# The experts' weighted products go to a buffer in SBUF and are summed in a step of their own, and the steps are put in another order

## The reference

```python
xn = layernorm(x)
# attention: 16 heads of 64, rotary embedding on q and k, causal mask
q, k, v = split(xn @ W_qkv)
q, k = rotary(q), rotary(k)
attn = softmax(where(mask, q @ k.T / 8, -1e9)) @ v @ W_out
# second block: 16 heads of 8 without a mask, then a gated choice among 8 experts
q, k, v = xn @ Wq + bq, xn @ Wk + bk, xn @ Wv + bv
h = xn + layernorm(softmax(q @ k.T / sqrt(8)) @ v @ Wo + bo, g1, be1)
gate = softmax(h @ Wg + bg)                 # 8 probabilities a row
top_vals, top_idx = top_k(gate, 2)
all_out = einsum('bsd,edf->bsef', h, We) + bexp
moe = sum(top_vals * all_out[top_idx])      # two experts a row
out = x + attn + (h + layernorm(moe, g2, be2))
```

## Time and profile before

| | us |
|---|---|
| three runs | 1206.92, 1212.21, 1213.35 |
| median | 1212.21 |
| the profiled execution, its own time | 1212.86 |
| its span on the core | 1211.0 |
| mean granted PE clock of the span, share of full speed | 0.963 |

### The profile page before, as it was taken

The page is one execution under the profiler, slowest core; times in us unless marked ns, Lnnn a source line. Parts: engine busy times, 40 slices in busy tenths (PEclk is TensorE's granted clock), DMA queues, the critical chain, the costliest instruction groups (busy, mean ns, idle before and its releaser), DMA issues.

```text
span 1211.0 us, 24662 instructions
## 1 busy us (share of the span) xinstructions
PE 1086.8 (90%) x8858; PEld 680.9 (56%) x8858; DVE 858.8 (71%) x2267; ACT 828.8 (68%) x1761; POOL 816.2 (67%) x753
## 2 busy tenths in 40 slices
PE   4688989999898998999988899998999999899996
PEld 3255656556574565756556455654656556565465
DVE  6666686766768568775879758786687776668557
ACT  4487766686657767588674877658776687566772
POOL 2675867587665688577775877649578568755780
PEclk9698999999889999999999999999999999699999
DMA  6112221122111132022211122112221122112111
GB/s 186 41 47 60 68 60 59 54 66 92 45 45 60 47 89 69 27 69 86 76 35 37 60 86 86 32 46 81 69 69 40 51 61 81 30 48 58 66 41 33
DMA packets 64741, 74.30 MB, mean 61 GB/s; under 512 B 22374, under 2 KB 34408, under 8 KB 64620
## 3 DMA queue, kind: packets, MB, share of 16 engines
q1 hardware_dynamic: 61148, 69.79, 18.6%
q10 hardware_dynamic: 3472, 2.95, 0.8%
HBM read 22.64 MB, written 3.67 MB: 22 GB/s over the span
## 4 chain that ended last, share of the span: by engine, by line
PE 63%; ACT 13%; DVE 12%; issue 4%; DMA 2%; POOL 2%; SPq 1%; ACTq 0%; POOLq 0%; DVEq 0%
PE work L1744 11%; PE work L1729 8%; PE work L1756 8%; PE work L1794 7%; DVE fnmax L1496 7%; PE work L1651 6%; ACT fpt L1334 5%; PE work L1653 5%; PE work L1652 5%; ACT pn L1389 4%; PE work L1766 4%; PE work L1775 4%; PE work L1784 3%; PE work L1655 1%; ACT raw L1359 1%
## 5 line engine op out<-in xcount | busy, mean ns | idle before, releaser
L1496 DVE TENSOR_REDUCE fnmax<-work 128x2 fp32r<-128x1024 f32 x256 | 302.3, 1218 | 82.4 <-PE work L1775 81.4
L1231 POOL TENSOR_TENSOR raw<-raw,cos_t 128x512 f32<-128x512 f32 x128 | 164.2, 1283 | 278.1 <-DMA swapped<-raw 275.7
L1389 ACT ACTIVATE pn<-work,nmax 128x512 f32<-128x512 f32 (+3 forms) x512 | 265.4, 537 | 73.8 <-DVE nmax L1609 69.8
L1609 DVE CUSTOM_DVE_ANT_0 work<-work,causal 128x512 f32<-128x512 f32 (+3 forms) x512 | 237.6, 517 | 107.9 <-PE work L1729 107.4
L1334 ACT ACTIVATE fpt<-work 128x1024 f32<-128x1024 f32 x256 | 251.0, 1028 | 76.3 <-PE work L1784 68.6
L1744 PE MATMUL work<-consts,pn 128*128 128x128 f32 x1280 | 182.1, 288 | 16.2 <-ACT fpt L1334 5.7
L1744 PEld LDWEIGHTS work<-consts,pn 128*128 128x128 f32 x1280 | 148.8, 147 | 61.3 <-DVE fnmax L1496 16.6
L1401 ACT COPY pt<-work 128x1024 f32<-128x1024 f32 x128 | 128.9, 1018 | 62.8 <-PE work L1744 62.6
L1235 POOL TENSOR_TENSOR raw<-raw,swapped 128x512 f32<-128x512 f32 x128 | 163.8, 1279 | 10.0
L1246 POOL TENSOR_TENSOR qk_l<-raw,qk_h 128x512 fp32r<-128x512 f32 x128 | 163.1, 1282 | 2.7
L1232 POOL TENSOR_TENSOR swapped<-swapped,sin_t 128x512 f32<-128x512 f32 x128 | 164.3, 1284 | 0.0
(11 more groups left out here) (153 smaller groups left out, 1790.4 us busy)
## 6 DMA issues: line engine op xcount, KB each, us to landing
swapped<-raw SPq DMA_DIRECT2D x256, 128.0 KB, 2.1
l_wide<-l_turned SPq DMA_DIRECT2D x128, 128.0 KB, 2.9
fqs<-fqn SPq DMA_DIRECT2D x96, 128.0 KB
x_in<-in_L_attn_x_dram SPq DMA_DIRECT2D x8, 256.0 KB, 3.9
out_dram<-x_in SPq DMA_DIRECT2D x7, 256.0 KB, 2.5
fpt<-in_L_attn_W_qkv_dram ACTq DMA_DIRECT2D x3, 512.0 KB, 6.4
l_turned<-l_inv SPq DMA_DIRECT2D x64, 16.0 KB
pt<-in_L_ffn_We_dram ACTq DMA_DIRECT2D x1, 512.0 KB, 9.6
```

Of the source, the lines that this page charges most:

```text
L1231: nc.gpsimd.tensor_tensor(raw[:, n % 3], raw[:, n % 3], cos_t[:], ALU.mult)
L1389: ins = nc.scalar.activation(pn[:, h, PN_AT[j]:PN_AT[j] + n], bank_of(("sc", b, c, unit), h)[:, at:at + n], ACT.Exp, scale=-1.0, bias=nmax ...
L1496: nc.vector.tensor_reduce(fnmax[:, g % 2, j * GH + 2 * r:j * GH + 2 * r + 2].unsqueeze(2), bank_of(("fsm", b, g, j), 2 * r, 2).rearrange(" ...
L1609: ins = nc.vector.tensor_tensor_reduce(out=scores, in0=scores, in1=causal[:, S - n:S], scale=-1.0 / math.sqrt(DH), scalar=3.0e38, op0=ALU.add,
```

## The change

1. `moew` is split. The multiplication writes to a new tensor `products` in SBUF, and a new DVE step `msum` sums from there. `FREED` still says `"moe": "moew"`, so it is the multiplication that frees the two banks. There is one `products`: the next multiplication waits for the sum before it. The wait for `x2` moves to the first `msum`.
2. `fnmax` has one copy instead of two; the first `fmax` of a group waits for the landing of `mput` of the group before.
3. `frec` (the reciprocals of `fdiv`) is a view of `stats`; the statistics wait for the last `fdiv`.
4. Six small tensors become views of one, `columns`; the exponent -0.5 is one column, broadcast.
5. `PLACE` and `PSUM` have other numbers (this is most of the diff's lines). In the new order `moew` and `msum` of one tile stand next to each other, as multiplication and sum did.

```diff
-        [168, 171, 172, 173],        # PLACE, "moew", batch 0
+        [168, 172, 174, 176],
+    "msum": [
+        [169, 173, 175, 177],
...
-        singles = sb("singles", [P, 5])
+        columns = sb("columns", [P, 12 * T + 6])
+        scales = columns[:, 0:9 * T].rearrange("p (k n t) -> p k n t", k=3, t=T)
+        spread, shift, rstd = (scales[:, n] for n in range(3))
...
-        fnmax = sb("fnmax", [P, 2, STRIP], F32R)
+        fnmax = sb("fnmax", [P, STRIP], F32R)
...
-        frec = sb("frec", [P, T, GH])
+        products = sb("products", [P, E, D])
+        frec = stats[:, :, 0:GH]
...
+            divided = []
+
             def statistics(kind, n, src):
+                if divided:
+                    dve.wait_ge(done["fdiv"], divided[-1])
...
                     if j == 0:
-                        wait(dve, landed("mput", *ring(2, b, g, G)))
+                        wait(dve, landed("mput", *ring(1, b, g, G)))
...
+                    divided.append(COUNT[x_])
...
                 elif kind == "moew":
                     t = x_[2]
                     if t == 0:
-                        wait(dve, after("x2", b))
                         wait(dve, after("pick", b))
                     wait(dve, after("moe", b, t))
-                    products = bank_of(("moe", b, t), 0, 2).rearrange("p (e d) -> p e d", d=D)
-                    nc.vector.tensor_tensor(products, products, gate_w[:, t].unsqueeze(2).broadcast_to([P, E, D]),
-                                            ALU.mult).then_inc(dve_link, 1)
-                    dve.wait_ge(dve_link, link())
-                    nc.vector.tensor_reduce(branch[:, t].unsqueeze(2), products.rearrange("p e d -> p d e"),
-                                            AX.X, ALU.add).then_inc(done["moew"], 1)
+                    wait(dve, after("msum", *ring(1, b, t, T)))
+                    nc.vector.tensor_tensor(products[:], bank_of(("moe", b, t), 0, 2).rearrange("p (e d) -> p e d", d=D),
+                                            gate_w[:, t].unsqueeze(2).broadcast_to([P, E, D]), ALU.mult).then_inc(done["moew"], 1)
+                elif kind == "msum":
+                    t = x_[2]
+                    if t == 0:
+                        wait(dve, after("x2", b))
+                    wait(dve, after("moew", b, t))
+                    nc.vector.tensor_reduce(branch[:, t].unsqueeze(2), products[:].rearrange("p e d -> p d e"),
+                                            AX.X, ALU.add).then_inc(done["msum"], 1)
                 elif kind == "ln2":
-                    wait(dve, after("moew", b, T - 1))
+                    wait(dve, after("msum", b, T - 1))
```

More of the change, by code:

```diff
@@ L62 @@
         [0],
[L63 to L68, removed]
+        [80],
+        [218],
+        [355],
+        [496],
+        [637],
+        [778],
         [920],
@@ L73 @@
         [88],
[L74 to L79, removed]
+        [229],
+        [368],
+        [513],
+        [654],
+        [793],
+        [935],
     ],
     "tb": [
-        [4],
+        [3],
     ],
     "proj": [
[8 rows of a table removed]
[8 rows of a table added]
     ],
@@ L410 @@
         [145],
[L411 to L412 removed]
+        [274],
+        [403],
         [532],
@@ L439 @@
     "nm2": [
-        [209],
-        [369],
-        [453],
-        [581],
-        [711],
-        [888],
-        [1012],
+        [198],
+        [362],
+        [456],
+        [577],
+        [710],
+        [880],
+        [1010],
         [1037],
@@ L450 @@
         [0],
-        [12],
-        [102],
-        [233],
-        [381],
-        [491],
-        [611],
-        [730],
+        [26],
+        [96],
+        [234],
+        [384],
+        [490],
+        [626],
+        [744],
+    ],
+    "wl": [
+        [1, 6, 20],
     ],
@@ L461 @@
     ],
+    "strl": [
+        [3],
+    ],
     "turn": [
@@ L607 @@
         [139],
-        [266],
-        [394],
-        [519],
-        [646],
-        [775],
-        [901],
-        [995],
+        [272],
+        [400],
+        [533],
+        [661],
+        [793],
+        [925],
+        [1024],
     ],
@@ L617 @@
         [145],
-        [272],
-        [399],
-        [526],
-        [653],
-        [780],
-        [909],
-        [1001],
+        [276],
+        [406],
+        [538],
+        [669],
+        [800],
+        [932],
+        [1029],
     ],
     "x2l": [
-        [158],
-        [285],
-        [411],
-        [538],
-        [665],
-        [790],
-        [917],
-        [1014],
+        [157],
+        [287],
+        [418],
+        [550],
+        [681],
+        [811],
+        [940],
+        [1040],
     ],
@@ L637 @@
         [161],
-        [288],
-        [415],
-        [541],
-        [668],
-        [794],
-        [921],
-        [1017],
+        [292],
+        [422],
+        [553],
+        [685],
+        [815],
+        [945],
+        [1044],
     ],
@@ L761 @@
     "out": [
-        [86],
-        [154],
-        [191],
-        [246],
-        [298],
-        [378],
-        [426],
+        [83],
+        [148],
+        [190],
+        [241],
+        [299],
+        [377],
+        [424],
     ],
@@ L998, in build @@
         bg_rows = sb("bg_rows", [P, E])
-        singles = sb("singles", [P, 5])
+        columns = sb("columns", [P, 12 * T + 6])
+        scales = columns[:, 0:9 * T].rearrange("p (k n t) -> p k n t", k=3, t=T)
+        spread, shift, rstd = (scales[:, n] for n in range(3))
+        gmax, gsum, grec = (columns[:, n * T:(n + 1) * T] for n in range(9, 12))
+        power = columns[:, 12 * T:12 * T + 1].broadcast_to([P, T])
+        singles = columns[:, 12 * T + 1:12 * T + 6]
         spare, value_bias, warm = (singles[:, n:n + 1] for n in range(3))
@@ L1501, in _ @@
                     wait(dve, *(after("fmax", b, g, T - 1, r) for r in range(2)))
-                    nc.vector.transpose(fnmax[:, g % 2].bitcast(F32), fnmax[:, g % 2].bitcast(F32)).then_inc(done["fturn"], 1)
+                    nc.vector.transpose(fnmax[:].bitcast(F32), fnmax[:].bitcast(F32)).then_inc(done["fturn"], 1)
                 elif kind == "fdiv":
@@ L1506, in _ @@
                     wait(dve, after("fT", b, g))
-                    nc.vector.reciprocal(frec[:].unsqueeze(3), sums[:, :, :, FD:FVW]).then_inc(dve_link, 1)
+                    nc.vector.reciprocal(frec.unsqueeze(3), sums[:, :, :, FD:FVW]).then_inc(dve_link, 1)
                     dve.wait_ge(dve_link, link())
@@ L1512, in _ @@
                         ct[:, :, g * GH * FD:(g + 1) * GH * FD].rearrange("p t (f d) -> p t f d", d=FD),
-                        sums[:, :, :, 0:FD], frec[:].unsqueeze(3).broadcast_to([P, T, GH, FD]), ALU.mult).then_inc(done["fdiv"], 1)
+                        sums[:, :, :, 0:FD], frec.unsqueeze(3).broadcast_to([P, T, GH, FD]), ALU.mult).then_inc(done["fdiv"], 1)
+                    divided.append(COUNT[x_])
                 elif kind in ("cl", "x2l"):
```

543 lines of the change are left out of this document (269 added, 274 removed), and 446 rows, old and new, of tables (PLACE, PSUM).

## The result

The changed kernel takes 1218.25 us (median of 18 executions) where the kernel before takes 1209.8 us in the same comparison: a ratio of 1.0063, 95% interval 1.0041 to 1.0086. It is **slower** by 0.6%, 8 us. The profiled execution has a span of 1217.4 us against 1211.0 before.

A forecast was written before the change was run, and what follows sets the result against it. PE, busy for 90% of the span, was taken as the bound, so only its waits counted. 1212.9 (profiled) - 6.0 + 1.3 - 0.6 = 1207.6 us, said as 1207.0 against the median; range 1195 to 1221.

The forecast's parts named there:

- the single fnmax: Rival: each group's first DVE reduction waits for the one copy's transfer, 2.0 us each; 1223 us, chance 0.14.
- term 1: Expert stage: products in SBUF free banks 1.24 us earlier; 6.0 us less, bounds 0 to 8.7, moved reductions' cost 0.
- first sign of being wrong: Expert stage on DVE: a reduction of the products taking over 1.5 us would show the forecast wrong.
- Reading SBUF in strides is slow: Rival, expert sums on DVE: reading across takes 2.54 us, 1.3 more each; 1240 us, chance 0.04.
- The release of the banks: Expert stage: banks come free after the multiplication, not the sum; 6.0 us less, at most 8.7.
- the six waits: PE's waits for the sum of the experts' products, 6.6 us in all, of which 6.0 was called recoverable.
- The opening: First batch: third wl delays the ninth reduction to 42.0; first masks 1.3 us later, bounds -1 to +5.
- GpSimd's late start: Rival, opening: second swap lands late, first scores wait for a lo ending after 54.5; 1216 us, chance 0.08.
- The end: Last batch: other work fills DVE's 0.68 us idle before gate's result; 0.6 us less, bounds 0 and 0.68.
- The clock: Rival: the new order spares the clock dip at 1040 to 1050, 5.0 us and as much again; 1199, chance 0.20.

The follow-up runs named there:

- e1_turned: The changed kernel with products kept as 128 x 8, so the multiplication reads PSUM across and the sum reads SBUF along; 1187.9 us, ratio 0.9835 to the kernel before.
- the dose: e1_turned with an unused contiguous reduction of 576 elements behind each sum; 1219.3 us, ratio 1.0077 to the kernel before.
- e6: e1_turned with the table of places and banks of the kernel before; ratio 0.997 to the kernel before.
- e7: The kernel before, order and PSUM products kept, with one fnmax, frec in stats and one tensor of columns; ratio 1.0073 to the kernel before.
- e2: The changed kernel's order with products in PSUM, each sum directly behind its multiplication and freeing the banks; ratio 0.9985 to the kernel before.

## Why the prediction was wrong

**The measured time lies within the range, on the wrong side of no change.** That the range holds it is luck: its upper part was there for the single fnmax and for GpSimd, and neither came about. The step that failed is in term 1: "The one DVE operation of 1024 elements that reads and writes SBUF alone took 1.211 us against 1.228 us for the one on PSUM: 0.017 us less. 32 of them are 0.5 us of an engine with 29% idle, so I put 0." That row is a contiguous operation, and the sum reads across. It bounded the wrong thing: SBUF against PSUM, where the price lies in the distance of the addends (0.65 to 0.75 us at 16 bytes and more, under 0.02 between the two memories). The sum took 1.983 us, so 24.3 us of DVE came where 0 was put; over 1.5 us was the prediction's own first sign of being wrong. The rule of the Trainium skill that was weighed there (VectorE: DVE Perf Modes, section on the TRN2 errata), 58 cycles of fixed cost for SBUF against 120 for PSUM, does not show in these rows: 1.21 to 1.22 us contiguous out of SBUF, 1.22 out of PSUM.

The rival "Reading SBUF in strides is slow" had the mechanism and even the total nearly right: it took 1.3 us a sum and 32 us in all, where the runs show 0.758 and some 28. It had 4% and was left out of the range. Its own sentence, that a new buffer read across is just the case, should have weighed more: there was a rule for it, and no row against it, since the only strided rows were of PSUM.

**"An engine with 29% idle" is no cover here.** In the stage of the earlier trace rows DVE has no idle time but what it waits for PE. From the first multiplication to the fourth it takes 12.22 us in the changed kernel's batch 0 and 9.89 in e1_turned: three sums, 3 x 0.76. And DVE's idle time over the span did not shrink to take in the 25 us of added work: 332.3 us (span less busy) with the slow sum, 328.2 with the quick one. The two profiled spans differ by 29.1 us. By the first part of their pages PE is idle for 138.0 us of the one and 117.5 of the other (span less busy), 20.5 us more, and busy for 1079.4 against 1070.8 us with the same 8858 products:

```profile
PE 1070.8 (90%) x8858; PEld 671.7 (57%) x8858; DVE 860.1 (72%) x2267; ACT 827.4 (70%) x1761; POOL 817.6 (69%) x753
```

These 8.6 us are the clock: granted 0.969 in the mean against 0.977, and 1070.8 x 0.977 / 0.969 is 1079.6. It is so in the other executions too, 0.969 against 0.978, and 0.969 with the dose. In the changed kernel it falls, among other places, in batch 4's expert stage and just behind it, the first time while PE was busy for 7.1 of 10 us (the stretches; columns as in the earlier trace rows; 0.86 and 0.80 are means of stretches that hold some of both levels, 1.2 and 2.4 GHz):

```profile
790.00:800.00 10.00, 9.03 (x43) 6.66 (x42) 9.76 (x8) 5.09 (x8) 4.37 (x4) 1.00 0.01 2
800.00:810.00 10.00, 7.08 (x49) 4.53 (x51) 9.69 (x17) 3.63 (x7) 7.21 (x6) 0.86 0.20 79
810.00:820.00 10.00, 10.00 (x87) 5.88 (x82) 6.82 (x26) 6.40 (x21) 0.87 (x2) 0.80 0.07 20
```

Such stretches stand in e1_turned as well (0.83 at 770 to 780). That DVE holding PE up is what lowers the clock is argued from these figures; no run shows it by itself. So 24.3 us of DVE cost some 28 us of time: nearly whole, and the clock on top.

**The release of the banks: right, and too small in the new order.** I took 6.0 us, 8.7 at most. In the order before, e6 against e7, the ratios differ by 1.0%: 12 us, with the two intervals 7 to 18, so near the forecast at its low end (the two profiled spans differ by 5.6 us). In the new order, e1 against e2, it is 1.5%: 18 us, with the intervals 13 to 23, above the upper bound. PE's wait for the release there falls from 7.9 to 2.2 us ahead of fsm, and DVE's idle time ahead of multiplications from 12.9 to 6.5 us, ahead of `fmax` from 72.2 to 69.6. These the six waits did not hold: the bound counted PE's waits by their named releaser only. But e2 moved five sums as well, and how much of the 18 us is theirs stays open. That the tables were made for the early release explains why e2 has little from them; it is an argument, no run shows it by itself.

**The opening: mis-sized, and of no account.** First masks forecast 1.3 us later, found 4.1. Of this, wl took 1.97 us instead of 1.21, beside GpSimd, and it started at 41.35, 0.55 later than reckoned (40.8). So the ninth `fmax` came 1.2 us later than reckoned, and another 1.6 us came behind it, where the last four `fmax` waited for fsm, 2.46 us the first time. But by the first expert stage only 1.5 us of the 4.1 were left, and three runs with an earlier opening won nothing that can be told. Why the opening of the kernel before loses time ahead of the first expert stage in the new order stays open.

**GpSimd's late start:** the second rope at 40.97 (forecast 40.6), the lo that the first scores need ends at 56.2 (54.0), and they start at 58.34 without a wait for it. The rival did not come about.

**The single fnmax:** right for the new order; no wait of DVE for m_turned is in its trace. In the order before it costs 0.7%.

**The end:** the idle 0.68 us ahead of gate's result is gone, but 0.71 us came ahead of the first multiplication, so the 0.6 was not won. Four slow sums are 3.0 us of DVE there, of which the end shows 2.1: with quick sums DVE waits for PE again.

**The clock:** the deep stretch at 1040 is gone, as the rival had it; the mean is 0.969 after 0.963 in the profiled executions, which fits the 7.4 us by which PE is busy for less. Over the executions of the experiments the kernel before has 0.966 to 0.969, so little of this is the change's. It was not what decided.

## What to carry to other kernels

A buffer that moves from PSUM to SBUF must be laid out anew: an access pattern that is free in PSUM can cost 60% more in SBUF once neighbouring accesses lie 16 bytes apart (here 1.98 us for 1.22). Let the operation that still reads PSUM do the turning; here four changed lines turned a loss of 0.6% into a gain of 1.6%. And an engine's idle share covers nothing in the stage where it and the bounding engine wait for each other: count an added duration there whole, and test it with a dose, an operation of the same length whose result is not used.

## What the runs showed of the hardware

- A DVE reduction of 1024 floats out of SBUF: 1.21 to 1.22 us with the addends 4 or 8 bytes apart, 1.86 to 1.96 us at 16, 64, 512 and 528 bytes. Out of PSUM 1.22 us at both 4 and 512 bytes. A copy across took 1.25 us, along 0.69; beside GpSimd the copy across took 1.98.
- A DVE operation on two SBUF tensors and GpSimd's multiplications hold each other up: 1.23 us alone, 2.18 beside it. The Trainium skill, SBUF — State Buffer, section on the two separate sides, describes this as an exclusive lock on a shared pair of ports. The traces agree that both sides lose (2.18 us on DVE, up to 2.12 on GpSimd for 1.26); whether it is a lock no run here shows. The row of before, 1.211 us for we_l, fell into a pause of GpSimd (43.56 to 44.58 us), so a duration read from one trace need not hold in another order.
